# The second attention layer rewritten: own PSUM banks for scores and for turned probabilities, division after the value product

## The chip, the cores and the metric

The kernel runs on one core of a Trainium2 chip. The metric is the time of one execution on the device in microseconds (us). The engines are TensorE (PE, matmuls; PEld its weight loads), VectorE (DVE), ScalarE (ACT), GpSimd (POOL) and SyncE (SP, which issues the DMAs). Each runs its own list of instructions in order and waits on semaphores for the others. TensorE writes to PSUM, which VectorE and ScalarE can read; the rest lies in SBUF.

## The reference

Two layers of cross-attention over 16 entries of 128 rows with 512 features, in 32-bit floats. The first layer (attention with a multilayer perceptron behind it) is not touched. The second, cut to what matters:

```python
q = hidden_state @ Wq + bq                 # 16 entries of 128 rows x 512
k = encoder_hidden_state @ Wk + bk         # 8 key heads of 16
v = encoder_hidden_state @ Wv + bv
scores = jnp.einsum('bkgld,bksd->bkgls', q, k) * scale + mask    # 32 query heads, 4 to a key head
attn = jax.nn.softmax(scores, axis=-1)
out = jnp.einsum('bkgls,bksd->bkgld', attn, v)
x = out @ Wo + bo + hidden_state
return (x - mean(x)) * rsqrt(var(x) + EPS) * gamma + beta
```

`hidden_state` is what the first layer gives, `encoder_hidden_state` the context. For each entry there are 32 heads of 128 x 128 scores.

## The kernel before, in words

The program has three stages: `attention` with L = 0 (first layer), `mlp`, and `attention` with L = 1 (second layer, from about 858 us to the end). Products that need precision are done in three passes over rounded halves ("hi" and "lo": a tensor rounded to the matmul's format, and what is left), by `split_product` (L158). `Staging` brings the weights in through a ring; ScalarE writes their high halves, VectorE the low ones.

One function serves both attention layers. The steps of an entry are written as calls `do["exp"](b, s, r, j)` and so on, in one order for all engines (`prologue` L349, `first_round` L393, `second_round` L439, `all_entries` L511); each engine takes part in the steps that it has a function for, so the order of work on each engine is this one list. Entries overlap: while entry b is in its softmax, b + 1 is projected, b - 1 gets its output product, b - 2 its normalisation.

In the second layer an entry has two rounds r of 16 heads, and a round has four banks S[0] to S[3] of PSUM with four heads each. For a round:

- TensorE writes the scores of all four banks (L1119, 24 matmuls that run four at a time on strips of 32 rows).
- VectorE adds the mask and takes the row maxima in one operation per head (`mask`, L922 to L940, at L937), writing the masked scores to `pr`; that frees the bank.
- ScalarE takes exponentials with their row sums (`exp`, L784, at L792), one per head.
- VectorE takes reciprocals of the sums, 8 columns at a time (`normalise`, L942, at L948), and GpSimd multiplies the probabilities by them, one bank of four heads per instruction (L683 to L691, at L690), eight instructions per entry.
- TensorE transposes the probabilities into the same four banks S (`probs`, L1136, at L1146); VectorE copies banks 0 and 2 to `pT` (L954), ScalarE banks 1 and 3 (L800). The banks are thus used alternately for scores and for transposed probabilities. There is one `pT`.
- TensorE multiplies with the values into bank O (L1150); VectorE casts the result to the high half (L961) and subtracts for the low half (L963).

```python
                    pool.wait_ge(rec_ready, w.event("pair"))
                    for j in (2 * pair, 2 * pair + 1):
                        part = pr[slot][:, j, :].rearrange("p (h k) -> p h k", k=keys)
                        by = rec[slot][:, j * per_bank:(j + 1) * per_bank]
                        pool.tensor_tensor(part, part, by.unsqueeze(2).broadcast_to([P, per_bank, keys]),
                                           ALU.mult).then_inc(normed, 1)
```

The other steps: `turn` transposes the entry's rows (L1053; ScalarE's high half at L743, VectorE's low half at L851), `query` (L1066) and `context` (L1082) project, `turn_query` (L1097) and `turn_context` (L1106) transpose the projections, `output` (L1172) is the product with Wo, twelve matmuls; VectorE adds the residual (L972) and takes the moments by bn_stats and small steps on one column (`moments`, L994 to L1014, among them L1003), GpSimd takes the root by Newton steps (`root`, L702), VectorE normalises (L1031), GpSimd applies gamma and beta (`affine`, L714) and makes the residual (L699). SyncE loads and stores.

## Time and profile before

| | |
|---|---|
| median of 3 runs | 1234.41 us (1229.36 to 1235.71) |
| the profiled execution | 1230.13 us, span 1228.3 us |
| busy over the span | PE 88%, PEld 74%, DVE 59%, ACT 53%, POOL 33% |
| the chain that ended last | PE 55%, POOL 14%, DVE 12%, issue 11%, ACT 4% |

The span is the time from the first to the last instruction of the profiled execution; the execution's own time is 1.8 us longer. Shares over the whole span mix three stages; the rows below are taken by stage. In rows of groups the columns are line, engine, operation, output and inputs, shapes and count, then busy us, mean ns of one, idle us of the engine just before them and what ended it. In rows in order of time they are start, length, engine, line, operation. An instruction's length is from its start to its end; on an engine the next one may start a little before that end, so the time for which an engine is held is read from start to start. In the chain an "issue" row is time in which the engine waited for nothing that the profile shows.

### The profile page before, as it was taken

What the parts mean: (1) busy time and instruction counts of PE and PEld (TensorE: products, weight loads), DVE (VectorE), ACT (ScalarE), POOL (GpSimd) and SP (SyncE); (2) the same over time, 40 slices, a digit from 0 to 9 for tenths busy, and PEclk for the clock granted to TensorE, in tenths of its full rate; (3) what the DMA queues carried; (4) which work ended last, traced back from release to release, by engine and by line L of the source; (5) the groups of instructions that cost most, each with busy time, mean ns of one, the idle gap of its engine ahead of it and who ended that gap; (6) DMA issues with size and microseconds to landing.
All of it is one profiled execution on the core that took longest, in us unless ns stands there. A gap on an engine that the chain in (4) does not pass through costs nothing.

```text
span 1228.3 us, 27299 instructions
## 1 busy us (share of the span) xinstructions
PE 1082.4 (88%) x8912; PEld 910.8 (74%) x8912; DVE 720.4 (59%) x2795; ACT 655.0 (53%) x2188; POOL 405.3 (33%) x539
## 2 busy tenths in 40 slices
PE   5999999999999983999999999998488888888863
PEld 4788888888888873898998999997366666666642
DVE  4577777677777764721222222222389898888982
ACT  4455555555455543733333333333388787888871
POOL 1233333333333331100000000000047676767674
PEclk9999999999999997999999999999699999999996
DMA  6312211111112102610110110040311212111100
GB/s 252 89 38 74 64 45 45 45 45 45 45 47 72 41 10 61 223 52 1 53 51 4 47 51 24 28 121 30 90 49 47 65 45 64 47 62 54 56 18 18
DMA packets 65348, 71.09 MB, mean 58 GB/s; under 512 B 7056, under 2 KB 41104, under 8 KB 65296
## 3 DMA queue, kind: packets, MB, share of 16 engines
q1 hardware_dynamic: 65296, 70.42, 18.3%
q8 instruction: 30, 0.49, 0.2%
q14 instruction: 22, 0.18, 0.1%
HBM read 49.43 MB, written 20.97 MB: 57 GB/s over the span
## 4 chain that ended last, share of the span: by engine, by line
PE 55%; POOL 14%; DVE 12%; issue 11%; ACT 4%; DMA 2%; SPq 1%; POOLq 1%; DVEq 0%; ACTq 0%
PE J L162 31%; PE S L162 15%; POOL pr L690 9%; POOL stat L710 3%; DVE pr L937 3%; PE S L1146 3%; PE O L1161 2%; ACT pr L792 2%; PE S L1128 2%; DVE stat L991 2%; POOL fin L720 1%; DVE stat L989 1%; DVE res L972 1%; DVE V L895 1%; PE T L1103 1%
## 5 line engine op out<-in xcount | busy, mean ns | idle before, releaser
L690 POOL TENSOR_TENSOR pr<-pr,rec 128x512 f32<-128x512 f32 x256 | 260.9, 1040 | 395.2 <-DVE rec L948 395.2
L792 ACT ACTIVATE pr<-pr,nmax 128x128 f32<-128x128 f32 (+1 forms) x768 | 324.5, 428 | 21.0 <-DVE nmax L937 20.9
L937 DVE CUSTOM_DVE_ANT_0 pr<-S,madd 128x128 f32<-128x128 f32 (+1 forms) x768 | 205.3, 330 | 13.4 <-PE S L1128 9.3
L1322 ACT ACTIVATE g_m<-J,b_part_m 128x256 f32<-128x256 f32 x128 | 60.6, 474 | 217.9 <-PE J L162 217.9
L1146 PE MATMUL S<-ident,pr 128*128 128x128 f32 x1024 | 130.4, 276 | 20.2 <-DVE nmax L937 16.7
L792 ACT ACTIVATION_READ_ACCUMULATOR pr<-pr,nmax 128x1 f32 x768 | 147.0, 191 | 0.0
L1146 PEld LDWEIGHTS S<-ident,pr 128*128 128x128 f32 x1024 | 115.3, 142 | 32.8 <-POOL pr L690 25.7
L1299 POOL TENSOR_TENSOR resid_m<-resid_m,b_all_m 128x512 f32<-128x512 f32 x16 | 23.1, 1464 | 325.3 <-DMA resid_m<-in_x 325.3
L954 DVE COPY pT<-S 128x512 f32<-128x512 f32 x128 | 84.1, 685 | 7.3 <-PE S L1146 5.9
L800 ACT ACTIVATE pT<-S 128x512 f32<-128x512 f32 x128 | 71.9, 587 | 24.8 <-PE S L1146 24.8
L162 PE MATMUL J<-nT0hi_m,uphi_m 128*128 128x256 f32 x256 | 73.1, 286 | 9.7 <-DVE uplo_m L150 8.9
L162 PE MATMUL J<-hThi,wkhi 128*128 128x256 f32 x256 | 75.3, 294 | 3.9 <-DVE wvlo L150 3.9
L162 PE MATMUL J<-wqhi,hThi 128*128 128x512 f32 x128 | 56.6, 442 | 22.3 <-DVE hTlo L851 11.9
L162 PE MATMUL J<-nT0hi_m,uplo_m 128*128 128x256 f32 x256 | 72.7, 284 | 0.0
L162 PE MATMUL J<-nT0lo_m,uphi_m 128*128 128x256 f32 x256 | 72.6, 283 | 0.0
L743 ACT ACTIVATE hThi<-J 128x512 fp32r<-128x512 f32 x48 | 28.7, 598 | 82.1 <-PE J L1060 82.1
L162 PE MATMUL J<-hThi,wklo 128*128 128x256 f32 x256 | 72.1, 282 | 0.0
L162 PE MATMUL J<-hTlo,wkhi 128*128 128x256 f32 x256 | 72.0, 281 | 0.0
L162 PE MATMUL J<-nT1hi_m,uphi_m 128*128 128x256 f32 x256 | 71.8, 280 | 0.0
L162 PE MATMUL J<-nT1hi_m,uplo_m 128*128 128x256 f32 x256 | 71.6, 280 | 0.0
L162 PE MATMUL J<-nT1lo_m,uphi_m 128*128 128x256 f32 x256 | 71.5, 279 | 0.0
L937 DVE DVE_READ_ACCUMULATOR2_ANT nmax<- 128x1 f32 x768 | 64.1, 84 | 0.1
(189 smaller groups left out, 2831.1 us busy)
## 6 DMA issues: line engine op xcount, KB each, us to landing
staged<-in_L_xattn_mlp_w SPq DMA_DIRECT2D x16, 512.0 KB, 4.7
rows<-in_ctx SPq DMA_DIRECT2D x16, 256.0 KB, 2.8
rows<-in_x SPq DMA_DIRECT2D x16, 256.0 KB, 3.0
kept_c<-hThi SPq DMA_DIRECT2D x16, 256.0 KB, 2.6
kept_c<-hTlo SPq DMA_DIRECT2D x16, 256.0 KB, 2.8
kept_n<-n_out SPq DMA_DIRECT2D x16, 256.0 KB, 2.4
n_in<-kept_n SPq DMA_DIRECT2D x16, 256.0 KB, 3.7
resid_m<-in_x SPq DMA_DIRECT2D x16, 256.0 KB, 2.8
```

Of the source, the lines that this page charges most:

```text
L162: mm = nc.tensor.matmul(out, stationary(a, k), moving(b, k), start=first and k == 0 and (a, b) == PASSES[0], stop=last and k == chunks - 1 ...
L690: pool.tensor_tensor(part, part, by.unsqueeze(2).broadcast_to([P, per_bank, keys]), ALU.mult).then_inc(normed, 1)
L710: pool.tensor_tensor(to, in0, in1, op).then_inc(newton, 1)
L743: nc.scalar.activation(hT[0][:, :, of_kind[kind], :], J[j][:, :].rearrange("p (k r) -> p k r", k=KC), ACT.Copy).then_inc(hT_hi, 1)
L792: last = nc.scalar.activation(part, part, ACT.Exp, bias=nmax[slot][:, at], scale=-1.0, accum_out=den[slot][:, at])
L800: nc.scalar.activation(pT[:, j, :], S[j][:, :], ACT.Copy).then_inc(S_taken[j], 1)
L937: last = nc.vector.tensor_tensor_reduce(pr[slot][:, j, cols], S[j][:, cols], madd[s][:, :], -1.0, FAR, ALU.add, ALU.min, nmax[slot][:, j * ...
L954: nc.vector.tensor_copy(pT[:, j, :], S[j][:, :]).then_inc(S_taken[j], 1)
L991: nc.vector.scalar_tensor_tensor(y, t, 1.5, y, ALU.add, ALU.mult).then_inc(small, 1)
L1128: mm = nc.tensor.matmul(S[j][:, c * 256:(c + 1) * 256], QT[s][qh][strip, RC * r + c, :], k_ap, start=(qh, kh) == PASSES[0], stop=(qh, kh) ...
L1146: mm = nc.tensor.transpose(S[j][:, to * P:(to + 1) * P], pr[slot][:, j, q * P:(q + 1) * P], ident[:, :])
L1322: nc.scalar.activation(g[slot][:, :], J[j][:, 0:PR], ACT.Gelu_apprx_tanh, bias=b1_part[:, f, :]).then_inc(J_taken[j], 1)
```

## The change

The second layer gets a function of its own, `second_attention`; `attention` is called for the first layer alone. The first layer and the `mlp` are the same. Instead of one common list of steps, every engine has its own `period(b)` that says in which order it serves the entries b - 2 to b + 2; all waits are computed from the entry's number. What is computed differs in these things:

- An entry has eight steps k of four heads (k = 0 to 3 first round, 4 to 7 second). Scores have the four banks S to themselves; the transposed probabilities go through two further banks PT = (O, T), even steps to one (copied by VectorE), odd ones to the other (copied by ScalarE). The remaining two banks G take everything else in turns: projections, transposes, value product, output product. `pr` has eight buffers, `pT` two.
- GpSimd no longer normalises the probabilities. VectorE takes the reciprocal of the 16 sums of a round, each repeated 16 times, so that `rec` is 128 x 256 (`invert`). TensorE transposes it into G[r] (`inverse`), ScalarE copies it to `inv` (`spread`), then the value product goes into the same bank, and VectorE multiplies it by `inv` twice (`attended`): once in full into `an`, once rounded into the high half `aT[.][0]`. GpSimd subtracts for the low half.
- The output product is issued in two halves of six matmuls. The moments use bn_aggr.

SyncE's loads and stores, not shown, are the same transfers: rows, context halves and mask of entry b + 2, one store per entry. `turn`, `query`, `turn_query`, `context`, `turn_context`, `output`, `root`, `affine`, `norm` and `mask_max` do the arithmetic of before. VectorE's `turn` waits for ScalarE's `turn`. `scores(e, 0)` waits for VectorE's `turn_context` of that entry.

```diff
         attention(nc, top, staging, 0, ident, handed, banks, x, ctx_rows, key_mask, q_b0,
                   (kv_b0,), out_b0, post_w0, None, None)
         mlp(nc, top, staging, handed, S, J, x, b1, b2)
-        attention(nc, top, staging, 1, ident, handed, banks, x, ctx_rows, add_mask, bq,
-                  (bk, bv), bo, gamma, beta, out)
+        second_attention(nc, top, staging, ident, handed, banks, add_mask, bq, bk, bv, bo, gamma, beta, out)
 
 
...
+    S, G, O, T = banks
+    PT = (O, T)
...
+        pr = [sb(f"pr{k}", [P, 2 * RC, R]) for k in range(STEPS)]
+        den = [sb(f"den{r}", [P, RC * EIGHT]) for r in range(ROUNDS)]
+        rec = [sb(f"rec{r}", [P, RC * EIGHT, DH1]) for r in range(ROUNDS)]
+        pT = [sb(f"pT{r}", [P, SB, RC, 2, R]) for r in range(ROUNDS)]
+        an = [sb(f"an{r}", [P, RC * R]) for r in range(ROUNDS)]
+        inv = [sb(f"inv{r}", [P, RC * R]) for r in range(ROUNDS)]
...
+                def attended(e, r):
+                    if r == 0:
+                        wait(pool, out_full, e.count(1, -1))
+                    hi, lo = (t[:, RC * r:RC * (r + 1), :].rearrange("p c r -> p (c r)") for t in aT[e.s])
+                    pool.wait_ge(a_hi, e.count(ROUNDS, r + 1))
+                    pool.tensor_tensor(lo, an[r][:, :], hi.bitcast(F32), ALU.subtract).then_inc(a_ready, 1)
...
+                def period(b):
+                    if b.plus(-2).exists():
+                        root(b.plus(-2))
+                    if b.plus(-1).exists():
+                        attended(b.plus(-1), 1)
+                    if b.plus(-2).exists():
+                        affine(b.plus(-2))
+                    if b.plus(1).exists():
+                        residual(b.plus(1))
+                    if b.exists():
+                        attended(b, 0)
...
+                def spread(e, r):
+                    act.wait_ge(r_full, e.count(ROUNDS, r + 1))
+                    wait(act, a_hi, e.count(ROUNDS, r - 1))
+                    nc.scalar.activation(inv[r][:, :], G[r][:, 0:RC * R], ACT.Copy).then_inc(r_spread, 1)
...
+                def period(b):
+                    before, after = b.plus(-1), b.plus(1)
+                    if b.exists():
+                        exp(b, 0)
+                    if before.exists():
+                        copy(before, 7)
+                    if b.exists():
+                        exp(b, 1)
+                    if before.exists():
+                        spread(before, 1)
+                    if b.exists():
+                        exp(b, 2)
+                        copy(b, 1)
+                        exp(b, 3)
+                    if after.exists():
+                        turn_query(after)
+                    if b.exists():
+                        exp(b, 4)
+                        copy(b, 3)
+                        exp(b, 5)
+                    if after.exists():
+                        turn_context(after)
+                    if b.it is None and b.n == -1:
+                        for u in OUT:
+                            staging.take_hi(nc, act, u, targets[u])
+                    if b.exists():
+                        spread(b, 0)
+                        exp(b, 6)
+                        copy(b, 5)
+                    if b.plus(2).exists():
+                        turn(b.plus(2))
+                    if b.exists():
+                        exp(b, 7)
...
+                def invert(e, r):
+                    dve.wait_ge(exped, e.count(STEPS, SB * r + SB))
+                    nc.vector.reciprocal(rec[r][:, :, :], den[r][:, :].unsqueeze(2).broadcast_to([P, RC * EIGHT, DH1]))\
+                        .then_inc(rec_ready, 1)
+                def copy(e, k):
+                    r, j = k // SB, k % SB
+                    dve.wait_ge(p_full[0], e.count(SB, k // 2 + 1))
+                    nc.vector.tensor_copy(pT[r][:, j, :, :, :].rearrange("p c a k -> p (c a k)"), PT[0][:, :])\
+                        .then_inc(copied[0], 1)
+                def attended(e, r):
+                    dve.wait_ge(o_full, e.count(ROUNDS, r + 1))
+                    wait(dve, a_ready, e.count(ROUNDS, r - 1))
+                    dve.wait_ge(r_spread, e.count(ROUNDS, r + 1))
+                    nc.vector.tensor_tensor(an[r][:, :], G[r][:, 0:RC * R], inv[r][:, :], ALU.mult)
+                    if r == 0:
+                        wait(dve, out_full, e.count(1, -1))
+                    nc.vector.tensor_tensor(aT[e.s][0][:, RC * r:RC * (r + 1), :].rearrange("p c r -> p (c r)"),
+                                            G[r][:, 0:RC * R], inv[r][:, :], ALU.mult).then_inc(a_hi, 1)
...
+                def period(b):
+                    before, after = b.plus(-1), b.plus(1)
+                    if b.exists():
+                        mask_max(b, 2)
+                    if before.exists():
+                        copy(before, 6)
+                        invert(before, 1)
+                    if b.exists():
+                        mask_max(b, 3)
+                        copy(b, 0)
+                    if after.exists():
+                        query(after)
+                    if b.exists():
+                        mask_max(b, 4)
+                    if before.exists():
+                        attended(before, 1)
+                    if b.exists():
+                        mask_max(b, 5)
+                        copy(b, 2)
+                    if after.exists():
+                        turn_query(after)
+                        context(after)
+                    if b.plus(-2).exists():
+                        norm(b.plus(-2))
+                    if b.exists():
+                        mask_max(b, 6)
+                        invert(b, 0)
+                        copy(b, 4)
+                        mask_max(b, 7)
+                    if after.exists():
+                        turn_context(after)
+                    if b.it is None and b.n == -1:
+                        for u in OUT:
+                            staging.take_lo(nc, dve, u, targets[u])
+                    if before.exists():
+                        output(before)
+                    if after.exists():
+                        mask_max(after, 0)
+                    if b.plus(2).exists():
+                        turn(b.plus(2))
+                    if before.exists():
+                        moments(before)
+                    if b.exists():
+                        attended(b, 0)
+                    if after.exists():
+                        mask_max(after, 1)
...
+                def scores(e, r):
+                    if r == 0:
+                        pe.wait_ge(k_ready, e.count(1, 1))
+                    wait(pe, masked, e.count(STEPS, SB * r))
...
+                def probs(e, k):
+                    t = k % 2
+                    pe.wait_ge(exped, e.count(STEPS, k + 1))
+                    wait(pe, copied[t], e.count(SB, k // 2))
+                    for i in range(2 * RC):
+                        mm = nc.tensor.transpose(PT[t][:, i * R:(i + 1) * R], pr[k][:, i, :], ident[:, :])
+                    mm.then_inc(p_full[t], 1)
+                def inverse(e, r):
+                    if r == 0:
+                        wait(pe, a_hi, e.count(ROUNDS, -1))
+                    else:
+                        wait(pe, res_ready, e.count(1))
+                    pe.wait_ge(rec_ready, e.count(ROUNDS, r + 1))
+                    for c in range(RC):
+                        mm = nc.tensor.transpose(G[r][:, c * R:(c + 1) * R], rec[r][:, c * EIGHT:(c + 1) * EIGHT, :],
+                                                 ident[:, :])
+                    mm.then_inc(r_full, 1)
+                def values(e, r):
+                    pe.wait_ge(r_spread, e.count(ROUNDS, r + 1))
+                    for t in range(2):
+                        pe.wait_ge(copied[t], e.count(SB, 2 * r + 2))
+                    for a in range(2):
+                        for j in range(SB):
+                            mm = nc.tensor.matmul(G[r][32 * j:32 * (j + 1), 0:RC * R], V[e.s][:, j, a, :],
+                                                  pT[r][:, j, :, a, :], start=a == 0, stop=a == 1)
+                    mm.then_inc(o_full, 1)
...
+                def period(b):
+                    before, after = b.plus(-1), b.plus(1)
+                    if before.exists():
+                        probs(before, 7)
+                    if after.exists():
+                        query(after)
+                    if b.exists():
+                        probs(b, 0)
+                    if before.exists():
+                        inverse(before, 1)
+                    if b.exists():
+                        scores(b, 1)
+                        probs(b, 1)
+                    if before.exists():
+                        values(before, 1)
+                    if b.exists():
+                        probs(b, 2)
+                    if after.exists():
+                        turn_query(after)
+                        context(after)
+                    if b.exists():
+                        probs(b, 3)
+                    if before.exists():
+                        output(before, 0)
+                    if after.exists():
+                        turn_context(after)
+                    if b.exists():
+                        probs(b, 4)
+                    if before.exists():
+                        output(before, 1)
+                    if after.exists():
+                        scores(after, 0)
+                    if b.exists():
+                        inverse(b, 0)
+                        probs(b, 5)
+                        values(b, 0)
+                        probs(b, 6)
+                    if b.plus(2).exists():
+                        turn(b.plus(2))
```

## Rows read from the trace of the kernel before

**Rows 1.** Busy time by stretch: start and end, length, engines, granted clock, DMA share, GB/s.
```profile
1000.00:1050.00 50.00, 41.44 (x393) 31.71 (x392) 44.72 (x249) 41.12 (x181) 34.99 (x62) 1.00 0.15 45
1180.00:1182.00 2.00, 0.64 (x10) 0.27 (x3) 1.79 (x17) 1.69 (x10) 0.00 (x0) 1.00 0.00 0
1204.00:1206.00 2.00, 0.02 (x1) 0.00 (x0) 0.00 (x0) 0.60 (x1) 1.45 (x8) 0.50 0.00 0
```

**Rows 2.** The chain of waits in the second layer: start, us, what.
```profile
876.86 6.26 ACT pr L792 x32
...
1029.45 2.04 POOL pr L690 x2
...
1039.35 3.28 issue
1042.67 2.04 POOL pr L690 x2
...
1049.56 2.03 POOL pr L690 x2
```

**Rows 3.** Groups of instructions by shape, second layer, 940 to 1140 us.
```profile
L690 POOL TENSOR_TENSOR pr<-pr,rec 128x512 f32<-128x512 f32 x80 | 81.5, 1039 | 45.3 <-DVE rec L948 45.3
L937 DVE CUSTOM_DVE_ANT_0 pr<-S,madd 128x128 f32<-128x128 f32 x320 | 70.5, 287 | 3.0 <-issue 3.0
...
L948 DVE RECIPROCAL rec<-den 128x8 f32<-128x8 f32 x40 | 7.8, 194 | 0.0
...
L1003 DVE TENSOR_TENSOR stat<-stat 128x1 f32<-128x1 f32 x10 | 9.4, 941 | 0.3
```

**Rows 4.** The same view, first layer, 100 to 430 us, VectorE and ScalarE.
```profile
L937 DVE CUSTOM_DVE_ANT_0 pr<-S,madd 128x256 f32<-128x256 f32 x192 | 69.4, 418 | 3.3 <-PE S L1128 3.3
...
L948 DVE RECIPROCAL rec<-den 128x4 f32<-128x4 f32 x48 | 8.2, 170 | 6.5 <-ACT pr L792 6.5
...
L754 ACT ACTIVATE KT0hi<-J,bk_part 128x256 fp32r<-128x256 f32 x24 | 11.4, 475 | 28.8 <-PE J L162 28.8
```

**Rows 5.** The line L948 by itself, 60 to 470 us and 960 to 1180 us.
```profile
L948 DVE RECIPROCAL rec<-den x60: 166/168/179, 69.5 to 466.1; 128x4 f32<-128x4 f32 x60
...
L948 DVE RECIPROCAL rec<-den x44: 189/194/199, 961.9 to 1177.3; 128x8 f32<-128x8 f32 x44
```

**Rows 6.** TensorE in order of time, one entry of the second layer.
```profile
1034.49 0.60 PE L1060 MATMUL J<-ident,y_rows 128*128 128x128 f32 x4
...
1037.61 0.39 PE L1128 MATMUL S<-KT0hi,QT0hi 32*128 32x256 f32 x4 [0.78 <-ACT pT L800]
...
1038.52 1.07 PE L1167 MATMUL O<-pT,V 128*32 128x256 f32 x16
1039.53 0.50 PE L162 MATMUL J<-wqhi,hThi 128*128 128x512 f32 x1
...
1042.43 1.03 PE L1146 MATMUL S<-ident,pr 128*128 128x128 f32 x8
```

**Rows 7.** ScalarE in order of time, the same entry.
```profile
1046.44 0.60 ACT L766 ACTIVATE QT1hi<-T 128x512 fp32r<-128x512 f32 x1
1046.94 0.39 ACT L792 ACTIVATE pr<-pr,nmax 128x128 f32<-128x128 f32 x1
```

**Rows 8.** VectorE in order of time, the same entry.
```profile
1043.25 0.28 DVE L937 CUSTOM_DVE_ANT_0 pr<-S,madd 128x128 f32<-128x128 f32 x1
...
1044.94 0.68 DVE L868 TENSOR_TENSOR Qn<-J,bq_all 128x512 f32<-128x512 f32 x1
1045.54 1.28 DVE L954 COPY pT<-S 128x512 f32<-128x512 f32 x2
1046.74 0.19 DVE L948 RECIPROCAL rec<-den 128x8 f32<-128x8 f32 x1
```

**Rows 9.** The layer's first maxima on VectorE; its last output product in the chain.
```profile
875.90 0.28 DVE L937 CUSTOM_DVE_ANT_0 pr<-S,madd 128x128 f32<-128x128 f32 x1
...
1211.09 5.50 PE J L162 x12
```

More of the change, by code:

```diff
@@ L1191, in _, with __init__, plus, exists @@
                                               finish=finish, projected=projected))
+class Entry:
+    def __init__(self, n, it=None):
+        self.n, self.it, self.s = n, it, n % 2
+    def plus(self, d):
+        return Entry(self.n + d, self.it)
+    def exists(self):
+        return self.it is not None or 0 <= self.n < B
+    def count(self, per, more=0):
+        fixed = self.n * per + more
+        return fixed if self.it is None else self.it * (2 * per) + fixed
+    def uses(self, per):
+        fixed = (self.n // 2 + 1) * per
+        return fixed if self.it is None else self.it * per + fixed
+    def index(self):
+        return self.n if self.it is None else self.it * 2 + self.n
```

317 lines of the change are left out of this document (added).

## The prediction

> **What bounds the kernel now.** First I split the run by stage. The second layer runs from about 858 us to the end, and only it changes. In its steady stretch no engine is full: VectorE is busy 44.7 of 50 us, TensorE 41.4, ScalarE 41.1, GpSimd 35.0, at the full TensorE clock [rows 1]. Then the chain of waits: it stays on GpSimd. The products of probabilities and reciprocal at L690 come four times per entry, two instructions each, and between them the chain shows "issue", time in which it waits for the reciprocals of the next sums. The same row returns after 1049.56 - 1029.45 = 20.11 us, the length of one entry [rows 2]. So the layer is a ring through GpSimd's normalisation, not a full engine, and VectorE, at 44.72/50 x 20.11 = 18.0 us per entry, is the nearest to full. The question is what VectorE carries afterwards and how often it waits.
>
> **What goes.** GpSimd loses eight products of 1.04 us per entry [rows 3], 8.3 us. It keeps the root, affine and residual steps and gains two subtractions 256 wide, all of it off the path: the low halves are ready long before the output product asks for them. With GpSimd idle, VectorE's sum in the moments (L1003, 0.94 us for one column where a reciprocal of 8 takes 0.19 [rows 3]; GpSimd is in a product then) no longer waits, and bn_aggr replaces six small steps: about 1.5 us less on VectorE per entry. The value product is divided instead: two multiplications 256 wide from PSUM in place of a cast and a subtraction, same width, and no wait between them: 0.2 us less. Nothing is gained in the scores, exponentials or copies: 32, 32 and 8 as before.
>
> **What comes: the wide reciprocal.** It now writes 256 columns, each sum sixteen times, twice per entry, in place of four reciprocals of 8 columns. No row has that width. The rows bound it. An ordinary VectorE operation costs 418 - 287 = 131 ns for 128 more columns, 1.02 ns each [rows 3, 4]; at that rate it is 0.45 us. But the reciprocal itself takes 170 ns for 4 columns and 194 for 8 [rows 3, 4]: 6 ns a column, six times as much; with the medians 168 and 194, 6.5 [rows 5]. I take 6.2 ns: 194 + 248 x 6.2 = 1.74 us. The shortest of the one width against the longest of the other (166, 199) gives 8.3 ns a column and 2.25 us, the upper end; the lower end is 0.45. I take 1.74, since it is the operation's own slope. The engine is held 1.66 us of it (two copies hold it 1.20 us and are done at 1.28 [rows 8]). VectorE then has 18.0 - 1.5 - 0.2 - 0.44 (four held 0.11) + 3.32 = 19.2 us of work per entry; with 0.45 it would be 16.6.
>
> The Trainium skill (VectorE: DVE Perf Modes, section "First, the fixed hardware budget") says that the reciprocal is an iterative divide with a repeat count of 8. By eight cycles a column at the page's 0.96 GHz it would be an estimated 2.3 us, which the means of the rows contradict and only their extremes allow; the time would be some 1281 us (rival d).
>
> **What comes: the new waits.** The other new thing is a round trip: the sums' reciprocals are transposed on TensorE (inverse, two transposes) and copied by ScalarE (spread, 256 wide, 0.475 us [rows 4]) before the values may be multiplied into the same bank. In program order TensorE does inverse(b,0) behind scores(b+1,0), which waits for VectorE's turn_context. ScalarE does spread(b,0) ahead of exp 6, copy 5 and turn(b+2); VectorE does turn(b+2) ahead of moments, attended and mask 1. I lay out one period, from mask 2 at 0, with these holds: four maxima 0.845 (eight in 1.69), copy 0.60 [rows 8]; four exponentials 1.54, done at 1.64 (16 in 6.26 [rows 2]), ScalarE copy of 512 0.50, done at 0.60 [rows 7]; TensorE scores 0.91, values 1.01, query 2.90, four transposes 0.43, done at 0.60 [rows 6]; 0.05 for each hand-over (an estimate).
>
> VectorE: mask 2 to 0.85, copy 6 to 1.45, reciprocal 1 to 3.11, mask 3 to 3.95. TensorE's scores(b,1) can go only then: 4.1 to 5.0, transposes, values of the old round 5.4 to 6.5. VectorE meanwhile does copy 0, query and mask 4 (to 6.0), waits 0.55, attended to 7.25, mask 5, copy 2, turn_query, context, norm, mask 6 to 11.0, reciprocal 0 to 12.7, copy 4, mask 7 to 14.1, turn_context to 14.7. Then the trip: scores(b+1,0) 14.8 to 15.7; inverse done 16.15; spread to 16.6; exp 6 done 18.25; transposes 6 to 18.7; turn done 19.3; ScalarE's turn done 20.0. VectorE has only the output sum and mask 0 to do (to 16.7, with 0.6 of waiting for the scores) and stands 3.3 us. Then turn to 20.6, moments 22.1, attended 22.8, mask 1 23.6, and mask 2 again. The period is **23.6 us: 19.2 of work and 4.45 of waits**, against 20.11. ScalarE, about 17 us of work, stands in the same trip (from turn_context at 12.4 to the spread at 16.2) and cannot exceed it; TensorE has 17 us of work and most of its waits there.
>
> **The sum.** The first maxima start at 875.9 [rows 9]; the prologue's loads, splits and products are the same and in the same order. Turn and mask 1 follow: mask 2 of entry 0 at 878.2. Period 0 has no older entry, but a query at half clock: 21.7. Periods 1 to 13: 13 x 23.6 = 306.8. Period 14 has no turn(16) and so not the long wait: 19.8. Period 15 has no next entry: 16.0. Then copy, reciprocal, transposes, spread and values to the last output product, 5.3; from its start to the end 17.2 today (1228.3 - 1211.09 [rows 9]), less 0.5 in the moments, so 16.7. Sum 878.2 + 21.7 + 306.8 + 19.8 + 16.0 + 22.0 = 1264.5. The profiled execution is 1230.1 for a span of 1228.3, so 1266.3. The median of the runs shown, 1234.4, lies 4 us above that execution; I say 1267.
>
> **Rivals.**
> (a) *The clock falls in the trip.* From 13.4 to 23 in the period TensorE has about 4 us of work, with gaps up to 2.3 us. Before, the clock held with 0.64 us of work in 2 us, and was at half (1.2 of 2.4 GHz) after the gaps around 1204 [rows 1]. If it falls, the next query takes some 4.9 instead of 2.9 us (an output product of the same twelve matmuls took 5.5 at half clock [rows 9]), of which the reciprocal hides a part: about 1.5 us per period, 14 of them, 1288 us. For: the long gaps. Against: each gap is shorter than those of the rows.
> (b) *The reciprocal is cheap* (0.45 us): both lie in the path, but the chain then sticks at query, probs 0, values, and the wait for probs 4: the period laid out by the same holds is 22.0, and the sum 1241 us. For: 256-column operations of other kinds; against: its own two widths.
> (c) *Faster.* The mechanism is that GpSimd's ring really was the whole price: the reciprocal is cheap, and VectorE meets every operand in time except in the trip, which costs 3.3 + 0.6 us whatever else is. The period is 16.6 + 3.9 = 20.5, period 0 20.4, the last two and the tail some 5 us less: 1217 us. It decides where the period falls below about 21.2. Against it: two conditions, of which rows contradict the first.
> (d) *The reciprocal is dearer*, 8.3 ns a column and 2.25 us: 0.5 us more twice per period, both in the path, 14 periods, 1281 us. For: the longest of its rows; against: all the rest of them. The Trainium skill's page above would have it so.
> (e) *The change does not do what it says*, the sixteenfold reciprocal being held back: nothing in the diff allows that; no chance of its own.
>
> **How the numbers follow.** Forecast 0.55 (own range 1252 to 1281, from +-1 us in the period: hand-overs, moments, the reciprocal's slope). (d) 0.08 at 1281. (a) 0.13 at 1288. (b) 0.11 at 1241. (c) 0.08 at 1217. Something between (b) and (c) 0.05. A measurement of this kernel can tell about 0.5%, 6 us, from no change. The range 1238 to 1288 leaves out (c), the case between, half of (a). Faster: (c) and part of the case between, 0.10. Same: the rest of it and half of (b), 0.08. Slower 0.82.
>
> **What would show it.** Right: a reciprocal of 128x256 at about 1.7 us; the same VectorE line returning every 23 to 24 us; the longest VectorE wait per entry some 3.3 us, ended by ScalarE's turn (h_hi); ScalarE's longest ended by the two inverse transposes; GpSimd under half busy; VectorE the leader of the chain. The prediction is wrong if the reciprocal takes about 0.45 us, if the wait at the turn is under 1 us, or if the period is at 20 us or less; wrong by (a) if the granted clock of the layer's middle is below 1.

## The result and the profile after

| | before | after |
|---|---|---|
| median | 1235.06 us (1229.36 to 1235.78, 4 runs) | 1286.91 us (1284.96 to 1292.53, 4 runs) |
| ratio | | 1.0441, 95% interval 1.0402 to 1.0481 |
| profiled execution, span | 1230.1, 1228.3 us | 1286.6, 1284.8 us |
| one entry of the second layer, mean of twelve | 20.10 us | 24.74 us |

Slower was forecast, 1267 us. The loss is 52 us where 33 were forecast. The time lies outside the forecast's own range of 1252 to 1281 and at the very end of the wide one: under 1288 us as a time, but as a ratio to the kernel before just over it (1.0441, where 1288 to 1234.41 is 1.0434). The entry's length is read here, and for every run below, from VectorE's `turn`, the low half of the turned rows: twelve of its returns, to the last one.

Busy time by stretch after the change answers to [rows 1]; the columns are the same (start and end, length, engines, granted clock, DMA share, GB/s):

```profile
1000.00:1050.00 50.00, 39.03 (x325) 29.18 (x325) 39.71 (x191) 33.96 (x152) 16.11 (x38) 0.91 0.14 45
1050.00:1100.00 50.00, 39.01 (x324) 29.17 (x324) 38.64 (x181) 33.36 (x149) 15.22 (x35) 0.91 0.14 45
```

GpSimd has fallen from 35.0 to 16.1 of 50 us, as intended, but TensorE, VectorE and ScalarE are less busy too: they wait more. Per entry VectorE has 39.71/50 x 24.74 = 19.6 us of work, near the 19.2 of the forecast; the rest, 5.1 us, is waits where 4.45 were forecast. The clock column is what the forecast did not have: 0.91 where it was 1.00. The longest waits, 940 to 1180 us (engine, line waited for, sum, times, longest):

```profile
ACT inv L1452 <- PE J L1720: 69.4, 20, 4.1
POOL aT0lo L1375 <- DVE aT0hi L1568: 55.9, 10, 6.5
...
DVE hTlo L1502 <- ACT hThi L1416: 30.4, 10, 3.0
...
PE T L1710 <- ACT pr L1438: 22.6, 10, 2.3
...
DVE pT L1558 <- PE O L1710: 7.6, 10, 1.7
```

The round trip is the first row (ScalarE waits for the transposed reciprocals, up to 4.1 us) and the third (VectorE stands 3.04 us for ScalarE's turn). The second is GpSimd's wait for a high half, which costs nothing. The last, VectorE's copy 0 waiting for step 0's transposes, which stand behind the query on TensorE, is small but was not in the forecast: 0.76 us an entry on average, up to 1.7. The wide reciprocal by its line:

```profile
L1552 DVE RECIPROCAL rec<-den x32: 1742/1746/1750, 890.7 to 1262.0; 128x256 f32<-128x256 f32 x32
```

1.746 us: the 1.74 of the forecast. Now TensorE in order of time in one entry (start, length, engine, line, what, and in brackets the idle time before it), and the same stretch by windows:

```profile
1022.69 0.65 PE L1710 MATMUL T<-ident,pr 128*128 128x128 f32 x4 [2.30 <-ACT pr L1438]
1024.09 0.54 PE L162 MATMUL J<-wqhi,hThi 128*128 128x512 f32 x1 [0.74 <-DVE aT1hi L1568]
1024.42 0.63 PE L162 MATMUL J<-wqlo,hThi 128*128 128x512 f32 x1
...
1026.98 0.63 PE L162 MATMUL J<-wqlo,hThi 128*128 128x512 f32 x1
1027.41 0.59 PE L162 MATMUL J<-wqhi,hTlo 128*128 128x512 f32 x1
1027.84 0.39 PE L162 MATMUL J<-wqhi,hThi 128*128 128x512 f32 x1
...
1028.53 0.60 PE L1710 MATMUL O<-ident,pr 128*128 128x128 f32 x4
```
```profile
1020.00:1022.00 2.00, 0.40 (x4) 0.16 (x2) 0.94 (x2) 1.57 (x7) 0.00 (x0) 1.00 0.71 266
1022.00:1024.00 2.00, 0.65 (x4) 0.42 (x4) 1.74 (x9) 2.00 (x12) 0.00 (x0) 1.00 0.02 6
1024.00:1026.00 2.00, 1.91 (x5) 1.59 (x6) 2.00 (x18) 1.68 (x9) 1.57 (x6) 0.60 0.00 0
1026.00:1028.00 2.00, 2.00 (x6) 1.54 (x6) 2.00 (x3) 0.56 (x4) 1.45 (x8) 0.55 0.00 0
```

TensorE waits 2.30 us for ScalarE's last exponentials, does four transposes, waits 0.74 us for `attended`, and then the granted clock is 0.60 and 0.55 in the next two windows, so at its lower level of 1.2 GHz for most of them: nine of the query's matmuls start 0.43 us apart where the last three start 0.23 apart. The query takes 4.4 us instead of 2.9 [rows 6], and in every fourth entry more (see the end). That is rival (a), in every entry.

### The profile page after: what moved, and what is told of

It reads as the page before. It is cut to its first block and busy times, and to the rows that moved or that the text cites. A ratio compares the mean times of both kernels' runs of the same rounds, so it can differ in the third digit from the quotient of the medians.

```text
span 1284.8 us, 27299 instructions
## 1 busy us (share of the span) xinstructions
PE 1122.9 (87%) x8976; PEld 934.7 (73%) x8976; DVE 744.6 (58%) x2699; ACT 659.3 (51%) x2220; POOL 297.5 (23%) x443
## 5 line engine op out<-in xcount | busy, mean ns | idle before, releaser
L1438 ACT ACTIVATE pr<-pr,nmax 128x128 f32<-128x128 f32 x512 | 198.1, 393 | 5.1 <-DVE nmax L1545 5.1
L689 POOL TENSOR_TENSOR pr<-pr,rec 128x512 f32<-128x512 f32 x128 | 130.6, 1042 | 297.9 <-DVE rec L947 297.9
L791 ACT ACTIVATE pr<-pr,nmax 128x256 f32<-128x256 f32 x256 | 126.6, 501 | 3.6 <-DVE nmax L936 3.5
L1545 DVE CUSTOM_DVE_ANT_0 pr<-S,madd 128x128 f32<-128x128 f32 x512 | 115.2, 284 | 14.1 <-PE S L1700 10.3
L1438 ACT ACTIVATION_READ_ACCUMULATOR pr<-pr,nmax 128x1 f32 x512 | 98.6, 193 | 0.0
L936 DVE CUSTOM_DVE_ANT_0 pr<-S,madd 128x256 f32<-128x256 f32 x256 | 92.6, 418 | 7.6 <-PE S L1127 7.5
L1710 PE MATMUL T<-ident,pr 128*128 128x128 f32 x256 | 41.3, 285 | 34.3 <-ACT pr L1438 34.3
L1452 ACT ACTIVATE inv<-J 128x256 f32<-128x256 f32 x32 | 12.3, 384 | 100.7 <-PE J L1720 100.7
L1145 PE MATMUL S<-ident,pr 128*128 128x128 f32 x512 | 62.3, 276 | 0.0
L162 PE MATMUL J<-wqlo,hThi 128*128 128x512 f32 x128 | 61.8, 483 | 0.0
```

Of the source, the lines that this page charges most:

```text
L162: mm = nc.tensor.matmul(out, stationary(a, k), moving(b, k), start=first and k == 0 and (a, b) == PASSES[0], stop=last and k == chunks - 1 ...
L791: last = nc.scalar.activation(part, part, ACT.Exp, bias=nmax[slot][:, at], scale=-1.0, accum_out=den[slot][:, at])
L936: last = nc.vector.tensor_tensor_reduce(pr[slot][:, j, cols], S[j][:, cols], madd[s][:, :], -1.0, FAR, ALU.add, ALU.min, nmax[slot][:, j * ...
L1145: mm = nc.tensor.transpose(S[j][:, to * P:(to + 1) * P], pr[slot][:, j, q * P:(q + 1) * P], ident[:, :])
L1438: last = nc.scalar.activation(pr[k][:, i, :], pr[k][:, i, :], ACT.Exp, bias=nmax[k][:, i:i + 1], scale=-1.0, accum_out=den[r][:, at:at + 1])
L1452: nc.scalar.activation(inv[r][:, :], G[r][:, 0:RC * R], ACT.Copy).then_inc(r_spread, 1)
```

## The experiments

The theory after the result has two parts. The clock adds its cost to the laid-out ring; and the ring (the steps that wait for each other in a circle, once an entry) is made of the wide reciprocal, the trip through TensorE and ScalarE, and the order in which the engines take their work. Each run is of the changed kernel with the edit named; ratios are to the kernel before, in runs beside it. An entry is measured in the profiled execution, and the time also holds the first and last entries, so differences of twelve entries and of medians agree only roughly.

| kernel | one entry, us | median, us | ratio, interval |
|---|---|---|---|
| before | 20.10 | 1235.06 | |
| the change | 24.74 | 1286.91 | 1.0441 (1.0402 to 1.0481) |
| keep_clock | 23.98 | 1277.07 | 1.0379 (1.0322 to 1.0437) |
| narrow_reciprocal | 23.99 | 1281.37 | 1.0401 (1.0348 to 1.0453) |
| exp_first | 23.87 | 1280.59 | 1.0395 (1.034 to 1.045) |
| turn_late | 22.81 | 1266.75 | 1.0267 (1.0215 to 1.0319) |
| keep_and_narrow | 24.01 | 1277.68 | 1.037 (1.0335 to 1.0404) |
| keep_narrow2 | 22.44 | 1253.35 | 1.0148 (1.0125 to 1.0171) |
| no_division | 23.45 | 1267.39 | 1.0291 (1.0232 to 1.0351) |
| no_division_keep | 21.17 | 1231.51 | 0.9973 (0.995 to 0.9996) |
| all_three | 20.95 | 1250.35 | 1.0139 (1.0067 to 1.021) |
| early_inverse | 20.49 | 1238.09 | 1.0043 (1.0023 to 1.0063) |
| best_keep | 19.69 | 1214.01 | 0.9835 (0.9807 to 0.9862) |
| best_query | 19.24 | 1209.74 | 0.9785 (0.9751 to 0.9819) |
| best_wide | 20.82 | 1237.92 | 1.0023 (0.9998 to 1.0048) |

**The clock.** keep_clock gives TensorE something to do in the gap, sixteen transposes that nobody reads:

```diff
+                        wait(pe, copied[1], before.count(SB, 3))
+                        for i in range(16):
+                            nc.tensor.transpose(PT[1][:, i % 4 * R:(i % 4 + 1) * R], pr[6][:, i % 4, :], ident[:, :])
                         probs(before, 7)
```

> Sixteen transposes of 128 columns whose result nobody reads are put on TensorE between turn(b+2) and step 7's transposes, where it stood idle 2.3 us; the computation is unchanged. Theory of the two costs (laid-out schedule plus clock): the granted clock stays at 1.00 through the query, the twelve query matmuls take 2.9 us in place of 4.1 to 4.9, VectorE's wait before copy 0 (0.47 us) goes, the period falls from 24.7 us on average to 23.6 to 23.8, and the time by 13 to 17 us, to about 1271. Rival (the half clock is hidden behind the reciprocal of the old round): the clock rises and the time does not move, 1285 to 1289. Second rival (1.7 us of work is not enough to hold the clock): the granted clock still shows 0.5 in the query and nothing moves.

TensorE in this kernel, the same place of an entry, and a stretch of its busy time:

```profile
1016.34 1.91 PE L1754 MATMUL T<-ident,pr 128*128 128x128 f32 x16
1018.73 0.66 PE L1710 MATMUL T<-ident,pr 128*128 128x128 f32 x4 [0.47 <-ACT pr L1438]
1020.19 0.50 PE L162 MATMUL J<-wqhi,hThi 128*128 128x512 f32 x1 [0.81 <-DVE aT1hi L1568]
1020.52 0.40 PE L162 MATMUL J<-wqlo,hThi 128*128 128x512 f32 x1
```
```profile
1000.00:1050.00 50.00, 40.34 (x381) 30.53 (x381) 40.52 (x191) 35.15 (x154) 15.40 (x35) 1.00 0.13 45
```

The wait before step 7's transposes is 0.47 us instead of 2.30, the clock 1.00, the query 2.9 us, and the entry 23.98 us each time: work that computes nothing makes the kernel 10 us faster. That is less than the 13 to 17 us expected, and the entry is a little longer than the 23.6 to 23.8, but both rivals are out. The clock is worth 24.74 - 23.98 = 0.76 us an entry: the row of VectorE's copies waiting for TensorE (7.6 us over 10) is gone from this kernel, and its wait for the turn is still 3.0 us.

**The reciprocal.** narrow_reciprocal takes 16 columns on VectorE and lets GpSimd repeat them:

```diff
-                    nc.vector.reciprocal(rec[r][:, :, :], den[r][:, :].unsqueeze(2).broadcast_to([P, RC * EIGHT, DH1]))\
+                    nc.vector.reciprocal(few[r][:, :], den[r][:, :]).then_inc(few_ready, 1)
...
+                    wide = few[r][:, :].unsqueeze(2).broadcast_to([P, RC * EIGHT, DH1])
+                    pool.tensor_tensor(rec[r][:, :, :], wide, ones[:, :].rearrange("p (h d) -> p h d", d=DH1), ALU.mult)\
```

> VectorE takes the reciprocal of 16 columns only; GpSimd, which is idle two thirds of the time, repeats it to 256 columns (a product with ones, about 0.75 us). Same result. Reciprocal 128x16: about 0.25 us in place of 1.75. Theory of the two costs: of the two reciprocals per period only the second (ahead of copy 4 and mask 7) lies bare; the first is covered by the query at half clock, so the period falls by 1.4 to 2.0 us and not by 3, and the time by 18 to 28 us, to about 1264. Rival (VectorE's work alone sets the period): both count, 3.0 us a period, 1286.9 - 42 = about 1245. Rival (the round trip hides all of it): the time moves by less than 8 us.

Both operations by their lines in this kernel:

```profile
L1564 DVE RECIPROCAL few<-den x32: 241/244/251, 892.2 to 1253.9; 128x16 f32<-128x16 f32 x32
```
```profile
L1402 POOL TENSOR_TENSOR rec<-few,ones x32: 612/622/632, 892.6 to 1257.2; 128x256 f32<-128x256 f32 x32
```

The operations shrank as meant and the time hardly did, 5.5 us where 18 to 28 were expected: a miss, in the range of the rival that named less than 8 us. In its place stand a wait of VectorE's copies for TensorE (27.5 us over 20 of them) and the query at the half clock. With the idle transposes added, keep_and_narrow:

> Both edits of before together: the sixteen idle transposes, and the 16-column reciprocal repeated by GpSimd. Same result. Alone they took 0.76 and 0.74 us off the mean period of 24.74. Theory (the query at half clock and the first reciprocal lie beside each other, each hiding the other, and behind them the laid-out schedule holds): together more than the sum, a period of 22.2 to 22.6 us (22.0 laid out for a short reciprocal, plus the 0.4 by which the full-clock period was over its 23.6), and about 1252 us. Rival (independent costs): 1.5 us, 23.2 us, about 1266. Rival (a third wait takes over): 24.0 us as with either.

It missed too: the entry stayed at 24.0 us, as the rival said in which a third wait takes over. The kernel's own waits say which (GpSimd's repeat is what TensorE waits for):

```profile
PEld J L1731 <- POOL rec L1402: 15.9, 10, 1.6
PE J L1731 <- POOL rec L1402: 13.6, 10, 1.4
```

My repeat stood behind GpSimd's root in the queue: the instrument had built a wait of its own. keep_narrow2 moves it ahead of the root (and the other round's repeat ahead of the affine step):

> The second layer with the 16 idle transposes that keep TensorE's granted clock at 1.00 and with the narrow reciprocal (VectorE 128x16, GpSimd repeats it over the query's columns), as in the run before of the two together, but with GpSimd's repeating product put ahead of its own root and affine steps, where it stood behind them and held TensorE's inverse transposes for 1.4 us. Theory (the wide reciprocal costs its own 1.74 us less 0.24 in the ring of the turn, once nothing stands in the repeat's place): the period falls from 23.98 us to 22.2 to 22.6, the time to 1252 to 1257 us, and TensorE waits for GpSimd's repeat less than 0.5 us. Rival (the ring is set elsewhere, the reciprocal lies beside TensorE's work): the period stays at 23.8 to 24.0 and the time at 1275 to 1280 us.

22.44 us, and TensorE has no such row left. The width of the reciprocal costs 23.98 - 22.44 = 1.54 us an entry in this order, half of the 3.0 us by which VectorE's two got shorter. It is the price of the exchange: the narrow kernel has GpSimd's 0.62 us twice in its place.

**The order of the work.** exp_first puts ScalarE's exp 6 ahead of its copy of the spread reciprocals:

```diff
-                        spread(b, 0)
                         exp(b, 6)
+                        spread(b, 0)
```

> One swap in ScalarE's order: exp 6 ahead of spread(b,0), so that the exponentials run in the 3.7 us in which ScalarE waits for the inverse. Same result. By the laid-out schedule the trip to turn(b+2) then hangs on the values and the copies and not on exp 6: VectorE's wait at the turn falls from 3.0 us to about 2.3, the period by 0.7 us, the time by about 10 us, to 1277. Rival (exp 6 is the trip's long piece and the trip is the period's): 1.5 us a period, 1265. Rival (VectorE only waits elsewhere): no change.

The waits moved as expected: the wait for the turn is 2.4 instead of 3.0 us and the entry 0.87 us shorter, at 23.87. The time fell by 6 us, not by ten. turn_late puts VectorE's turn, whose wait held mask 1 up, behind it:

```diff
-                    if b.plus(2).exists():
-                        turn(b.plus(2))
...
                         mask_max(after, 1)
+                    if b.plus(2).exists():
+                        turn(b.plus(2))
```

> One move in VectorE's order: turn(b+2) from ahead of moments, attended and mask 1 to behind them, so that 3.05 us of work fill the 3.04 us in which VectorE stood. Same result. By the laid-out schedule the wait at the turn all but goes, and step 7's exponentials and transposes, and with them the query, come up to 0.9 us later than VectorE would like: 2.1 us less per period at full clock, and up to 3 with the shorter gaps in TensorE's work keeping its clock; the time falls by 30 to 42 us, to 1245 to 1257. Rival (the wait is not at the turn but in the ring, whatever the order): less than 10 us.

The direction is right, 1.9 us an entry and 20 us of the time, but the expectation was for more: TensorE's wait of 2.3 us for the exponentials is unchanged (22.6 us over 10), with the clock at 0.93 and 0.97 in the two stretches of 50 us. no_division takes away everything that the division asks for, reciprocals, inverse transposes and spreading; the value products are multiplied by ones, so the softmax's division is left out:

> The division is left out altogether: no reciprocals, no inverse transposes, no spread; the values are multiplied by a tile of ones. What is left is the new layer's banks and order alone. Theory (reciprocals and the round trip are the loss, the new order by itself no gain over the old layer): laid out by the same holds, the trip is only scores, values, transposes and turn, and the period 20.4 to 20.9 us at full clock, 21.5 if the query still runs at half; time 1230 to 1245, which is no better than the kernel before, that does divide. Rival (the order would be good and the division alone spoils it): below 19 us a period, 1210 or less.

Another miss: 20.4 to 21.5 us were expected, and without any division the new layer still has 23.45 us an entry. Its query by the first of three products, and the same with the idle transposes added, no_division_keep (min, median and max in ns):

```profile
L162 PE MATMUL J<-wqlo,hThi x40: 388/628/632, 951.5 to 1166.2; 128*128 128x512 f32 x40
```
```profile
L162 PE MATMUL J<-wqlo,hThi x46: 388/394/398, 945.8 to 1179.4; 128*128 128x512 f32 x46
```

> The second layer without any division (no reciprocals, no inverse transposes, no spreading; the value products are multiplied by ones, so this kernel leaves the softmax's division out) and with the 16 idle transposes ahead of step 7's. Theory (the clock is the larger part of what the new order costs without its division: the query's matmuls took 649 ns each at the half clock, 5.25 us, where they take some 2.9 at full): the period falls from 23.85 us to about 21.5, the time from 1267 to 1235 to 1245 us, at a granted clock of 1.00 in the layer's middle. Rival (the ring is closed by waits and not by the clock): the query becomes short, the wait for the turn longer by as much, and the period stays above 23.3, the time above 1260 us.

The median falls from 628 to 394 ns and the entry to 21.17 us, a little better than expected. So the loss of 4.64 us an entry has three parts: the new order at full clock 21.17 - 20.10 = 1.07 (against a kernel that does divide), the division in it 23.98 - 21.17 = 2.81 (1.54 of it the width), the clock 0.76. The parts depend on what else is there: with no division the clock costs 23.45 - 21.17 = 2.28.

**Put together.** all_three joins the narrow reciprocal, exp_first and turn_late:

> Narrow reciprocal, exp 6 ahead of the spread, VectorE's turn behind mask 1. Same result. Theory: the first removes 3 us of work and the others the wait at the turn, so the period is 20.5 to 21.5 us and TensorE's gaps get short enough to keep its clock for most periods; 1230 to 1245 us. Rival (step 7's exponentials, last on ScalarE, hold the next query and so the ring): 22 us or more, 1255.

The entry came out as expected, 20.95 us; the time did not, 1250.35 us for 1230 to 1245.

early_inverse has the narrow reciprocal and the late turn, and takes TensorE's inverse transposes from behind the next entry's scores:

```diff
+                    if b.exists():
+                        if after.exists():
+                            pe.wait_ge(k_ready, after.count(1, 1))
+                        inverse(b, 0)
                     if after.exists():
                         scores(after, 0)
                     if b.exists():
-                        inverse(b, 0)
                         probs(b, 5)
```

with the context's transposition ahead of the output product on TensorE, and its copies earlier on ScalarE and VectorE.

> Narrow reciprocal, VectorE's turn late, and the context's transposition ahead of the output product on TensorE, behind exp 4 on ScalarE and behind mask 6 on VectorE, so that the bank G[0] is free for inverse(b,0) before scores(b+1,0) instead of behind it. Same result. Theory (ScalarE's 3.7 us before the spread is the trip's root): ScalarE's wait for the inverse of round 0 all but goes, the period is 20 to 21 us, the time 1225 to 1240. Rival (mask 7 and copy 4 only take the trip's place): as without it, about 1260.

It holds: 20.49 us an entry and 1238.09 us. Its longest wait on TensorE is still the old one, and of its entries every fourth or so takes 21.9 us, with a half clock in the query:

```profile
PE T L1723 <- ACT pr L1450: 27.0, 12, 2.3
```

best_keep fills that gap with the idle transposes; best_query fills it with the query itself. Both have GpSimd's repeat ahead of its root. best_query needs three more moves, so it differs from best_keep by more than the filling: ScalarE's copy 7 goes behind exp 1, VectorE's turn back ahead of mask 1, and the first round's values ahead of step 5's transposes.

```diff
                     if after.exists():
                         query(after)
+                    if before.exists():
+                        probs(before, 7)
```

> The early-inverse kernel with GpSimd's repeat ahead of its root and with the 16 idle transposes ahead of step 7's, in place of the moved query. Theory (what every fourth period of 21.9 us holds above the others' 20.0 is the clock alone): all periods about 19.8 us, granted clock 1.00, about 1225 us. Rival (the dummy transposes cost what the clock gives back, or the long periods have another cause): 1236 to 1240 us as without them.

> The early-inverse kernel (narrow reciprocal, turn behind the first mask, the context's transposition ahead of the output product, the next entry's inverse transposes ahead of its first scores), with GpSimd's repeat ahead of its root, and with TensorE's query product put ahead of step 7's transposes, so that it fills the 2.3 us in which TensorE waited for the last exp; ScalarE and VectorE take their steps in the order that this asks for. Theory (the 2.3 us of TensorE's wait and the half clock behind it are what is left above the old layer): a period of 19.3 to 20.0 us, no half clock in the query, and 1215 to 1228 us, faster than the kernel before. Rival (the wait only moves, the query now waits for the turned entry or the copies behind it are late): a period of 20.3 us or more, 1235 us or more.

Both theories hold and both kernels are faster than the numbers said: 1214.01 us for about 1225, and 1209.74 for 1215 to 1228. best_query by windows and waits:

```profile
1000.00:1050.00 50.00, 45.06 (x419) 35.01 (x420) 42.84 (x243) 45.11 (x200) 21.51 (x53) 1.00 0.17 53
1050.00:1100.00 50.00, 43.89 (x399) 33.66 (x398) 41.47 (x231) 42.31 (x188) 22.78 (x44) 0.97 0.21 67
```
```profile
PE J L162 <- DVE hTlo L1516: 19.3, 11, 1.8
DVE pT L1571 <- PE O L1724: 14.5, 21, 2.4
```

TensorE's wait for the last exponentials is gone; what it waits for is the turn, 1.8 us, and the clock drops only now and then. It is 2.2% faster than the kernel before and 6% faster than the change. Last, the same order with the change's own wide reciprocal, best_wide:

> The fastest kernel so far (late turn, early inverse transposes, the query ahead of step 7's transposes) with the change's own wide reciprocal on VectorE put back, and GpSimd's repeat taken out: only the order of the work differs from the change. Theory (in the change the width costs 1.54 us an entry, since one of the two reciprocals hides behind other engines' work; the same half is exposed in the better order): the period rises from 19.2 to 20.7 to 21.0 us and the time from 1210 to 1232 to 1238 us, level with the kernel before, so the order alone takes back all that the change lost. Rival (with the waits gone VectorE is the nearest to full, 16.5 us of work an entry and 3.0 more with the wide ones, so that both are exposed): a period of 22.0 to 22.4 us, 1250 to 1258 us.

```profile
1000.00:1050.00 50.00, 41.94 (x395) 31.25 (x394) 46.11 (x216) 39.92 (x176) 19.12 (x37) 1.00 0.15 51
```

1237.92 us, as expected: the order alone takes the loss back to nothing that can be told from the kernel before in the time. Its entry is still 0.72 us longer than before (20.82 for 20.10). Again half of the width is exposed (20.82 - 19.24 = 1.58), though VectorE is busy 46.1 of 50 us and has the least left of all engines.

## Why the prediction was off

**What held.** The direction; the ring through GpSimd gone (16.1 of 50 us); the reciprocal at 1.746 us (194 + 248 x 6.2 is 1.73, not the 1.74 written), on its own slope from two narrow widths, the 16 columns at 0.244 lying on the same line, (1746 - 244)/240 = 6.26 ns a column; VectorE's waits of 3.04 us at the turn (3.3), 0.74 for the scores (0.6) and 0.60 before `attended` (0.55); ScalarE's longest wait ended by the inverse transposes; the tail of 17.0 us (16.7). With 0.24 us of reciprocal and the repeat the ring at full clock has 22.44 us, near the 22.0 laid out for the cheap one. The Trainium skill (VectorE: DVE Perf Modes, "First, the fixed hardware budget") gives the reciprocal a repeat count of 8; the estimate of eight cycles a column made from it, some 2.3 us, is not borne out by the measured 1.746. That VectorE leads the chain can't be read: the chain of this execution goes back only into the tail.

**The step that failed** is the query taken at the full clock, 2.90 us, in the laid-out period, and with it the claim that VectorE comes from mask 3 to copy 0 without a wait; the clock's fall in the trip stood as rival (a) only. I saw the gap of up to 2.3 us (it is 2.30), named the consequence (a query of 4.9 us; it is 4.4) and the place, and then gave it 0.13, because each gap was shorter than those in [rows 1] that had lost the clock. Measured, most of the query runs at the half clock in every entry and copy 0 waits 0.76 us on average. keep_clock shows the mechanism: nothing but the gap was filled. It should have been a term of the forecast. Its size was mis-stated as well, 1.5 us an entry for a measured 0.76: VectorE is in the wide reciprocal and mask 3 while the query runs, from 1026.24 to 1028.7 us in the entry shown, which hides the rest. That the median came so near to the 1288 of rival (a) is in part luck: its clock term was double the measured one, and the ring and the ends, which it had too short, make up for that. The condition written down for it, a granted clock below 1 in the layer's middle, is met: 0.91.

**A term mis-sized** is the laid-out ring: 23.98 us at full clock for 23.6. In keep_clock's entry from 1020.89, where mask 2 starts, mask 4 is done at 6.24 (laid out 6.0), VectorE's turn starts at 20.26 (20.0) and mask 1 is done at 24.14 (23.6): a quarter of a microsecond is lost before mask 4 in hand-overs, as much again in the moments, which take 1.76 us from the row statistics to `attended` where 1.5 was said. The mean over the twelve is 0.38.

**The ends** were too short. The first maximum starts at 876.73 us for 875.9 and mask 2 of entry 0 at 879.01 for 878.2, 0.8 late; keep_clock, whose edit starts only behind this, has 875.85, so that is this execution's own. Entry 0 took 23.5 us for 21.7. From mask 2 of entry 14 to the last output product it is 45.1 for 19.8 + 16.0 + 5.3 = 41.1, and from there to the end 17.0 for 16.7. The sum: 0.8 and 1.8 at the start, 320.2 - 306.8 = 13.4 for the thirteen entries between, 4.0 and 0.3 at the end make the 20.3 us between the forecast's span of 1264.5 and 1284.8.

keep_clock's trace tells which of these are the clock. Its entry 0 is 23.5 us as well, so that excess is not the filled gap; what it is stays open. Its thirteen take 311.1 us, and from mask 2 of entry 14 to the end it has 58.7 where the change has 62.1 and the forecast 57.8. So the gap and the clock make 9.1 us of the thirteen and 3.4 at the end, and the ring as laid out is short by 4.3. These are the profiled executions, 13.5 us apart; the medians of the two kernels are 9.8 apart. Without the clock's loss in each entry, the median of 1277.07 us lies in the forecast's own range of 1252 to 1281.

## What to carry to other kernels

When a change opens a gap on TensorE, even of two microseconds, ask what it runs next: if that is a long product, price it at the half clock in the forecast itself, and try to put the product into the gap. An operation moved onto another engine's path is cheap or dear by its place in each queue: here the same work took 24.74 or 20.82 us an entry. An instrument is queued too; look at its own waits before its verdict is believed.

## What was not expected of the hardware

Sixteen transposes that compute nothing made the kernel 10 us faster in the change, and 36 us without the division (1267.39 to 1231.51). The granted clock fell with TensorE partly busy: 0.40 and 0.65 us of work in two windows of 2 us, then 0.60. Before the change 0.64 us of work in 2 us had not brought it down [rows 1]; what tells the two cases apart no run here shows.

And every fourth entry of the change, exactly, was 1.3 us longer (25.7 for 24.4). In such an entry the granted clock stays at its lower level through the whole query, whose matmuls start 0.43 us apart to the last, and VectorE's copy 0 waits 1.70 us where it waits 0.40 in the entry shown above:

```profile
1072.00:1074.00 2.00, 1.26 (x4) 0.99 (x4) 2.00 (x16) 1.68 (x8) 1.08 (x3) 0.55 0.00 0
1074.00:1076.00 2.00, 2.00 (x7) 1.52 (x6) 2.00 (x8) 1.29 (x8) 1.37 (x9) 0.50 0.00 0
1076.00:1078.00 2.00, 2.00 (x6) 1.52 (x5) 1.50 (x9) 0.00 (x0) 0.57 (x3) 0.50 0.00 0
```
```profile
1029.17 0.69 DVE L1558 COPY pT<-O 128x512 f32<-128x512 f32 x1 [0.40 <-PE O L1710]
...
1079.19 0.69 DVE L1558 COPY pT<-O 128x512 f32<-128x512 f32 x1 [1.70 <-PE O L1710]
```

keep_clock has no such beat, 23.98 us in each, so it belongs to the clock; why it is the fourth entry each time is open.
